# Delta stage of a two-layer kernel: the decay's distance as an absolute value on ScalarE, with work orders of their own for prologue and last head

## The chip, the cores and the metric

One core of one Trainium2 chip runs the whole program in one launch. The metric is the time of an execution in microseconds; three runs of the kernel before were timed, and one more was taken with the hardware profiler. Times inside the program are microseconds from the start of the profiled span.

## The reference

The program computes two transformer layers for B = 2 sequences of S = 512 rows with D = 256 columns, all in float32. Each layer adds a mixer and a mixture of experts, each behind a layer norm. The change touches only the first mixer, a gated delta rule with 16 key heads and 32 value heads of 128:

```python
mixed = silu(causal_conv1d(x @ w_qkv, conv_w))      # 4 taps
q, k, v = split(mixed)                              # q, k l2-normalised, each shared by 2 value heads
g = -exp(A_log) * softplus(x @ w_a + dt_bias);  beta = sigmoid(x @ w_b)
St = St * exp(g_t)                                  # one step per row t
delta = (v_t - k_t @ St) * beta_t
St = St + outer(k_t, delta);  o_t = q_t @ St
out = (rmsnorm(o) * norm_weight * silu(x @ w_z)) @ w_out
```

The kernel does it in chunks of 128 rows. Inside a chunk it needs, for rows j <= i, the decay exp(G_i - G_j), where G is the running sum of g (which is never positive, so that G falls with the row). As a full 128x128 matrix with both signs of the distance turned to the same one this is exp(-|G_i - G_j|): the mask of the later products throws away the half that isn't wanted.

## The kernel before

`build` (L2194) runs its phases one after the other: norm and gates (`phase_norm`, `phase_gates`, which also writes the running sums G of all heads to DRAM as rows), then `phase_delta` (L399), then the experts, attention and the second experts. Each phase is a block in which every engine has its own in-order program, and semaphores tie them together.

In `phase_delta` a head (one key head with its two value heads, both sequences; U = 4 units) passes through two halves. The preparation: eight convolutions (`conv` on TensorE, read out by `conv_r`, L785, as one plain and one scaled copy on ScalarE, three taps `tapa`, `tapb`, `tapc`, L926, on VectorE, `silu`, L794, on ScalarE), transposes `queries`, `keys`, `vals` with their read-outs, sums of squares `qsq` and `ksq` (four squares each), the gate products `gate`, the scalars `nscal` (L677) on GpSimd, and per chunk c = 0 to 3 the decay: `row` (L616) on SyncE fetches G of the chunk broadcast to all partitions (256 KB), `gap` (L710) turns it into the distance, `dexp` (L843) into the decay `dT`, `gram` multiplies keys with keys and queries, `mt` and `at` (VectorE) take the decay in, `cm` (GpSimd) and `nl` (VectorE) apply scale and mask, and `am` (GpSimd) masks `dT`. The 16x16 diagonal blocks of `nl` go through DRAM to a layout of lanes (`gath`, `gathr`), are inverted there in 13 steps `lane0` to `lane12` on VectorE, and come back (`putx`, `puty` behind a transposed copy `yl` on ScalarE, `scaty`, `scatx`). The second half, the recurrence: three levels of merges of the blocks (`v`, `m`, `y`, `a`, `xa`, `xb`), and per chunk `recall`, `rhs`, `solve`, `dl`, `ds`, `update`, `st`, `recallq`, `qs`, `output`, `o`, then norm and projection (`square`, `factor`, `oz`, `corev`, `core`, `core_r`, `project`, `project_r`). Stages without an engine named here are TensorE's if they are products, and else VectorE's or ScalarE's copies.

The order in which each engine runs its stages is written out by hand in one table `WINDOW` (L334) of 230 names. An engine's program is this table with only its own stages kept, so moving a name moves that stage on its one engine, and the distance between names of different engines means nothing. The table pairs the recurrence of head H with the preparation of head H + 1. It is used 15 times; the prologue (head 0's preparation, `PRO`) is the table with only preparation stages, the last head (`LAST`) with only recurrence stages (L375). In the last head every `v` and `y` starts with four idle products of 256 columns. Two PSUM banks `pp` go round among all users of `BANK_USERS` in the table's order, so a stage that takes a bank waits until the one two turns before is read out. At the start of each window SyncE's `head` (L595) waits until the window before has filled its last bank, then fetches the weights of head H + 2 (776 KB) and an output weight, and then come the four `row`.

The distance is two GpSimd operations per chunk, over 128x512: subtraction (L717) and a product with a table of signs (L719):

```python
pool.tensor_tensor(d, rows[p][:], over(hs[s][:, GRID, units(c)], 2, P), ALU.subtract).then_inc(s_gap, 1)
pool.wait_ge(s_gap, 2 * (CH * at.PH + c) + 1)
pool.tensor_tensor(d, d, over(k.c(C_SIGN), 1, U), ALU.mult).then_inc(s_gap, 1)
```

The weights of head 0 and 1 are fetched at the start of `phase_delta` (L590, L591), ahead of the first rows, which also wait until GpSimd has cleared 13 tiles (`s_zero`).

## Time and profile before

| | |
|---|---|
| three runs, median (lowest to highest) | 1699.26 us (1699.21 to 1701.25) |
| the profiled execution, own time | 1702.14 us |
| its span, mean granted TensorE clock | 1700.3 us, 0.953 of full speed |
| busy: TensorE, VectorE, GpSimd, ScalarE | 93%, 72%, 53%, 51% |
| delta stage | from about 39.5 to 1226 us |

The page gives each engine's busy share of the whole span; the prologue, the windows and the last head have different limits, so the timeline and the waits are read stretch by stretch. A timeline row gives start, duration, engine, line, operation, written and read tiles, shapes and how many instructions were merged into the row; in brackets the idle time before it and what ended it. "issue" means that no releaser was found. Matmul durations contain the pipeline's latency: stages follow each other faster than the durations add up, so the time of a stage is read from its start to the next one's.

### The profile page before, as it was taken

Reading aid. Unit: us, or ns where it says so; the run is one execution under the profiler, and the core shown is the slowest. Engines: PE = TensorE matmul, PEld = TensorE weight load, DVE = VectorE, ACT = ScalarE, POOL = GpSimd, SP = SyncE. Lnnn points to the kernel's source line nnn. Section 1 sums busy time; section 2 is a strip of 40 time slices with the busy share of each in tenths; the row PEclk is TensorE's granted clock in tenths of the full one; section 3 lists DMA queues with packets and bytes.
Section 4 is the critical chain, followed back from the end, with each engine's and each line's share of the span. In section 5 each row is a group of like instructions: output and inputs, shape, how many; then the busy total and the mean of one; then the engine's idle time right before and its main releaser. Section 6 shows DMA issues by size and latency. Waiting matters only on the chain. (4 is left out here: it accounts for less than half of the span.)

```text
span 1700.3 us, 28667 instructions
## 1 busy us (share of the span) xinstructions
PE 1587.0 (93%) x9280; PEld 1168.9 (69%) x9280; DVE 1216.5 (72%) x2565; ACT 860.2 (51%) x2367; POOL 908.4 (53%) x1101
## 2 busy tenths in 40 slices
PE   2689999999999999999999999999899899997997
PEld 2368778777787777877778777777655455555675
DVE  5679888898897978989788788894354354434445
ACT  1646757667576675766757667572311123341121
POOL 1647668686676866768668686672400112231332
PEclk8889999999999999999999999999999977778999
DMA  1120220201202012020120201200021360000413
GB/s 51 60 67 10 59 55 20 62 14 55 59 16 62 14 55 61 14 62 14 54 61 14 62 15 53 49 8 12 1 81 38 130 232 1 1 1 10 147 53 109
DMA packets 128642, 82.58 MB, mean 49 GB/s; under 512 B 92304, under 2 KB 110992, under 8 KB 128368
## 3 DMA queue, kind: packets, MB, share of 16 engines
q1 hardware_dynamic: 125152, 73.52, 15.4%
q0 software_dynamic: 2256, 6.18, 1.0%
q8 instruction: 78, 1.28, 0.3%
q10 hardware_dynamic: 1088, 1.05, 0.2%
q14 instruction: 68, 0.56, 0.1%
HBM read 62.97 MB, written 17.74 MB: 47 GB/s over the span
## 5 line engine op out<-in xcount | busy, mean ns | idle before, releaser
L926 DVE SCALAR_TENSOR_TENSOR dr_acc<-dr_raw,dr_wh,dr_acc 128x512 f32<-128x512 f32 x384 | 363.5, 960 | 46.1 <-ACT dr_acc L792 42.1
L1138 PE MATMUL dr_pp<-xnT,dr_wh 128*128 128x512 f32 x512 | 243.5, 609 | 6.0 <-DMA dr_wh<-in_w_head 5.4
L1138 PEld LDWEIGHTS dr_pp<-xnT,dr_wh 128*128 128x128 f32 x512 | 93.1, 194 | 88.6 <-issue 72.1
L1218 PEld LDWEIGHTS dr_pI<-dr_V,dr_X 128*64 128x64 f32 (+1 forms) x1536 | 125.3, 156 | 40.4 <-issue 30.5
L717 POOL TENSOR_TENSOR dr_dT<-dr_rows,dr_hs 128x512 f32<-128x512 f32 x64 | 76.5, 1195 | 134.2 <-issue 119.6
L1200 PEld LDWEIGHTS dr_pI<-dr_Y,dr_nl 128*64 128x64 f32 (+1 forms) x1536 | 125.5, 156 | 17.9 <-issue 13.5
L1170 PE MATMUL dr_pp<-dr_wh,xnT 128*128 128x256 f32 x512 | 124.5, 387 | 12.6 <-DVE x L1118 6.6
L1218 PE MATMUL dr_pI<-dr_V,dr_X 128*64 128x64 f32 (+1 forms) x1536 | 134.5, 242 | 0.2 <-DVE dr_V L1056 0.2
L1200 PE MATMUL dr_pI<-dr_Y,dr_nl 128*64 128x64 f32 (+1 forms) x1536 | 132.4, 240 | 1.7 <-DMA dr_Y<-dr_blocks_y 1.5
L791 ACT ACTIVATE dr_raw<-dr_pp 128x512 f32<-128x512 f32 x128 | 75.9, 593 | 107.2 <-PE dr_pp L1138 68.1
L1290 PE MATMUL dr_pp<-dr_wo,xn 128*128 128x256 f32 x512 | 124.3, 386 | 3.6 <-issue 1.8
L744 POOL TENSOR_TENSOR dr_ds<-dr_dl,dr_hs 128x512 f32<-128x512 f32 x48 | 62.4, 1299 | 120.4 <-ACT dr_dl L892 120.4
L756 POOL TENSOR_TENSOR xn<-xn,dr_zs 128x512 f32<-128x512 f32 x64 | 95.7, 1496 | 43.6 <-DVE xn L1113 34.0
L1170 PEld LDWEIGHTS dr_pp<-dr_wh,xnT 128*128 128x128 f32 x512 | 95.8, 193 | 29.7 <-DVE x L1118 10.1
L1960 POOL TENSOR_SCALAR_AFFINE_SELECT at_pT<-at_pT 128x128 f32<-128x128 f32 x128 | 36.1, 292 | 143.6 <-ACT at_pT L2107 142.3
L1290 PEld LDWEIGHTS dr_pp<-dr_wo,xn 128*128 128x128 f32 x512 | 94.3, 192 | 18.6 <-ACT xn L908 5.4
L719 POOL TENSOR_TENSOR dr_dT<-dr_dT,cst 128x512 f32<-128x512 f32 x64 | 94.7, 1480 | 5.0
L900 ACT ACTIVATE xn<-xn 128x128 f32<-128x128 f32 x256 | 75.7, 297 | 34.2 <-POOL dr_fac L770 19.1
L2107 ACT ACTIVATE at_pT<-at_u 128x512 f32<-128x512 f32 (+3 forms) x128 | 50.7, 444 | 73.7 <-PE at_u L2025 73.4
L732 POOL TENSOR_TENSOR dr_dT<-dr_dT,cst 128x512 f32<-128x512 f32 x64 | 80.8, 1283 | 13.0 <-DVE dr_dT L967 13.0
L792 ACT ACTIVATE dr_acc<-dr_pp,dr_wh 128x512 f32<-128x512 f32 x128 | 87.1, 680 | 0.0
L2015 PE MATMUL at_u<-at_kT,at_qT 32*128 32x512 f32 (+3 forms) x256 | 83.5, 583 | 0.2 <-DVE at_mx L2153 0.2
(292 smaller groups left out, 3736.3 us busy)
## 6 DMA issues: line engine op xcount, KB each, us to landing
dr_rows<-gt_rows SPq DMA_DIRECT2D x64, 256.0 KB, 3.5
dr_wh<-in_w_head SPq DMA_DIRECT2D x16, 776.0 KB, 4.6
ex_w<-in_moe SPq DMA_DIRECT2D x18, 608.0 KB, 11.1
dr_wo<-in_w_out SPq DMA_DIRECT2D x16, 256.0 KB, 4.7
dr_sorted_x<-ex_zero SPq DMA_DIRECT2D x1, 3999.0 KB, 29.5
so_xt<-dr_sorted_x SPq DMA_DIRECT2D x3, 1032.0 KB, 9.3
m_w<-in_moe SPq DMA_DIRECT2D x8, 384.0 KB, 3.1
dr_blocks_l<-dr_nl SPq DMA_DIRECT2D x128, 16.0 KB, 1.7
```

Source lines behind the costliest of these rows:

```text
L717: pool.tensor_tensor(d, rows[p][:], over(hs[s][:, GRID, units(c)], 2, P), ALU.subtract).then_inc(s_gap, 1)
L719: pool.tensor_tensor(d, d, over(k.c(C_SIGN), 1, U), ALU.mult).then_inc(s_gap, 1)
L732: pool.tensor_tensor(d, d, over(k.c(C_LE), 1, U), ALU.mult).then_inc(s_am, 1)
L756: pool.tensor_tensor(core[:].rearrange("p (b v) d -> p b v d", b=B), o[:].rearrange("p (b v) d -> p b v d", b=B), z, ALU.mult).then_inc(s_ ...
L792: act.activation(acc[q][:], flat(ps), ACT.Identity, scale=wh[at.ps][:, tap:tap + 1]).then_inc(free, 1)
L926: dve.scalar_tensor_tensor(acc[q][:], raw[q][:, w:w + S], wh[at.ps][:, col:col + 1], acc[q][:], ALU.mult, ALU.add).then_inc(done[q], 1)
L1138: mm = pe.matmul(flat(ps), wh[at.ps][:, w0:w0 + P], k.xnT[:, kt, b * S:(b + 1) * S], start=(kt == 0), stop=(kt == KT - 1))
L1170: mm = pe.matmul(ps[:, 2 * a:2 * a + 2].rearrange("p a b -> p (a b)"), k.xnT[:, kt, n * P:(n + 1) * P], wh[at.ps][:, w0:w0 + REP * DH], st ...
L1200: mm = pe.matmul(pairs(h, s)[rows, u], above(g, l), odd(Y[at.s][:, g:g + 1], s)[:, 0], start=True, stop=True)
L1218: mm = pe.matmul(pairs(h, s)[rows, u].rearrange("p m s -> p (m s)"), left[:, h * HU + u], V[h][:, u], start=True, stop=True)
L1290: mm = pe.matmul(ps[:, 2 * b:2 * b + 2].rearrange("p a b -> p (a b)"), cT[:, REP * b + w], wo[s][:, w], start=(w == 0), stop=(w == REP - 1))
L2015: pe.matmul(ps[:, 0:(qt + 1) * P], qT[Q % 2][rows, t0:t0 + P], kT[Q % 2][rows, b * S:b * S + (qt + 1) * P], start=True, stop=True).then_in ...
```

## The change

`gap` moves from GpSimd to ScalarE: four activations of 128x128 with the absolute value, scale -1 and the column of G as bias, |G_i - row|, instead of the two GpSimd operations; the exponential takes the minus sign as its scale. The table of signs leaves the constants. `WINDOW` is written anew; `PRO` and `LAST` become tables of their own. The weights of head 0 are fetched in the first norm phase, with a tile that lives longer. Cut to the core (the new tables stand whole, of the old `WINDOW` the start and the end):

```diff
                 sp.dma_start(k.alog[:], a_log_dram.partition_broadcast(P)).then_inc(k.s_gates, 16)
+                sp.dma_start(k.wh0[:], w_head_dram[0]).then_inc(k.s_wh0, 16)
                 sp.dma_start(k.router0[:], router_dram.rearrange("(k p) e -> p k e", p=P)).then_inc(k.s_router0, 16)
...
+PRO = """
+scal row0 yz conv1 conv0 conv_r1 tapa1 tapb1 tapc1 row1 conv3 conv_r0 conv2 gap0 silu1 tapa0 tapb0 tapc0 conv_r3
+tapa3 tapb3 queries1 tapc3 silu0 conv_r2 queries0 qsq1 tapa2 silu3 qsq0 tapb2 keys1 tapc2 keys_r1 silu2 keys0 ksq1
+keys_r0 ksq0 nscal gap1 gram0 gram1 row2 cm0 dexp0 dexp1 mt0 conv5 at0 conv4 gram2 gap2 dexp2 mt1 row3 at1 mt2
+gram3 nl0 cm1 gap3 dexp3 nl1 mt3 conv_r4 cm2 cm3 conv_r5 nl2 nl3 tapa5 tapb5 at2 gate0 tapa4 gath tapb4 conv7 tapc5
+gate_r0 silu5 at3 conv_r7 tapc4 gate2 tapa7 am0 tapb7 gate3 gathr lane0 lane1 gate_r2 gate1 gate_r1 silu4 gate_r3
+lane2 lane3 lane4 am1 conv6 lane5 vals1 lane6 lane7 lane8 lane9 lane10 lane11 conv_r6 lane12 tapc7 yl tapa6 tapb6
+vals_r1 am2 putx silu7 puty scaty tapc6 vals0 silu6 vals3 vals_r0 vals2 vals_r3 vals_r2 am3 scatx
+""".split()
 WINDOW = """
-conv1 row0 scal conv_r1 row1 conv0 gap0 conv_r0 tapa1 tapb1 tapc1 tapa0 conv3 tapb0 gap1 v0 silu1 conv_r3 m0 row2
-tapc0 silu0 conv2 conv_r2 tapa3 dexp0 y0 tapb3 queries0 a0 qsq0 tapc3 xa0 v1 tapa2 v2 dexp1 m2 conv5 y2 row3 m1 y1
...
-dl3 output3 oz2 lane6 lane7 gate_r0 lane8 corev2 lane9 core2 project_r1 o3 oz3 lane10 gate2 lane11 core_r2 square3
-lane12 at2 gate_r2 project2 factor3 corev3 gate1 yl tapc7 putx puty project_r2 vals2 gate_r1 silu7 at3 core3
-vals_r2 vals3 am1 vals_r3 core_r3 project3 scaty am2 project_r3 scatx am3
+scal conv1 conv_r1 tapa1 row0 conv0 tapb1 conv_r0 conv3 tapc1 tapa0 silu1 tapb0 v0 m0 conv_r3 tapa3 gap0 tapc0 v1
+y0 dexp0 m1 a0 row1 conv2 gap1 v2 yz silu0 tapb3 row2 tapc3 xa0 m2 silu3 y1 conv_r2 keys1 y2 keys_r1 a2 a1 xa1
+conv5 ksq1 queries0 tapa2 conv_r5 tapb2 v4 m4 v3 xb0 y4 tapc2 row3 qsq0 m3 silu2 tapa5 y3 keys0 a4 a3 keys_r0
+solve0 dl0 ds0 gram0 queries1 output0 ksq0 tapb5 qsq1 mt0 gram1 update0 tapc5 dexp1 gap2 o0 at0 conv4 conv_r4 st0
+xb1 gap3 recall1 mt1 nscal dexp2 v5 rhs1 tapa4 recallq1 cm0 solve1 at1 m5 dl1 gram2 qs1 cm1 dexp3 tapb4 ds1 tapc4
+gram3 nl0 mt2 square0 conv6 silu4 nl1 update1 y5 cm2 silu5 mt3 st1 oz0 nl2 conv_r6 a5 cm3 nl3 factor0 gath output1
+o1 vals0 square1 recall2 rhs2 conv7 solve2 tapa6 vals_r0 at2 conv_r7 tapb6 dl2 gathr tapc6 recallq2 corev0 tapa7
+factor1 qs2 ds2 vals1 core0 output2 oz1 vals_r1 o2 update2 corev1 core_r0 project0 st2 core1 core_r1 project_r0
+recall3 square2 am0 recallq3 project1 lane0 lane1 rhs3 oz2 solve3 qs3 dl3 gate0 lane2 silu6 lane3 factor2 lane4
+project_r1 lane5 lane6 corev2 am1 lane7 gate_r0 lane8 am2 output3 o3 core2 gate3 core_r2 oz3 lane9 lane10 gate2
+gate_r3 lane11 lane12 project2 square3 tapb7 gate_r2 factor3 project_r2 tapc7 yl corev3 gate1 vals2 vals_r2 gate_r1
+silu7 core3 core_r3 vals3 putx puty vals_r3 project3 at3 scaty am3 scatx project_r3
+""".split()
+LAST = """
+v0 v1 m0 m1 y0 a0 y1 xa0 v2 a1 m2 y2 a2 v4 v3 xb0 xa1 m3 m4 y4 a4 y3 a3 solve0 dl0 ds0 v5 output0 update0 o0
+square0 m5 st0 recall1 rhs1 xb1 solve1 y5 dl1 ds1 recallq1 a5 update1 oz0 factor0 corev0 qs1 output1 st1 recall2 o1
+rhs2 recallq2 square1 core0 core_r0 solve2 project0 dl2 oz1 project_r0 ds2 update2 factor1 qs2 st2 output2 recall3
+corev1 o2 core1 oz2 rhs3 square2 factor2 core_r1 recallq3 solve3 qs3 dl3 corev2 output3 o3 core2 square3 project1
+project_r1 core_r2 oz3 project2 factor3 corev3 core3 project_r2 core_r3 project3 project_r3
 """.split()
...
             sp.dma_start(nw[:], norm_w_dram.rearrange("(p a) -> p a", a=1)).then_inc(s_nw, 16)
-            load_w(w_head_dram[0:1], 0)
             load_w(w_head_dram[1:2], 1)
...
                 sp.wait_ge(k.s_rows, 16)
-                wait(sp, s_gap, 2 * (CH * at.PH + c - 2) + 1)
+                wait(sp, s_gap, CH * at.PH + c - 1)
                 sp.dma_start(flat(rows[p]), k.rows_dram[at.PH, c].partition_broadcast(P)).then_inc(s_rows[p], 16)
...
 
-            def gap(at, c):
-
-                s, p = at.ps, c % 2
-                pool.wait_ge(s_hs, at.PH + 1)
-                pool.wait_ge(s_rows[p], 16 * (2 * at.PH + c // 2 + 1))
-                wait(pool, s_O, CH * (at.H - 1) + c + 1)
-                d = dT[s][:, c]
-                pool.tensor_tensor(d, rows[p][:], over(hs[s][:, GRID, units(c)], 2, P), ALU.subtract).then_inc(s_gap, 1)
-                pool.wait_ge(s_gap, 2 * (CH * at.PH + c) + 1)
-                pool.tensor_tensor(d, d, over(k.c(C_SIGN), 1, U), ALU.mult).then_inc(s_gap, 1)
-
             def cm_(at, c):
...
 
+            def gap(at, c):
+
+                s, p = at.ps, c % 2
+                act.wait_ge(s_hs, at.PH + 1)
+                act.wait_ge(s_rows[p], 16 * (2 * at.PH + c // 2 + 1))
+                wait(act, s_O, CH * (at.H - 1) + c + 1)
+                for u in range(U):
+                    own = hs[s][:, GRID, c * U + u:c * U + u + 1]
+                    ins = act.activation(dT[s][:, c, u], rows[p][:, u], ACT.Abs, bias=own, scale=-1.0)
+                ins.then_inc(s_gap, 1)
+
             def dexp(at, c):
-                act.wait_ge(s_gap, 2 * (CH * at.PH + c) + 2)
-                act.activation(dT[at.ps][:, c], dT[at.ps][:, c], ACT.Exp).then_inc(s_dt, 1)
+                act.wait_ge(s_gap, CH * at.PH + c + 1)
+                act.activation(dT[at.ps][:, c], dT[at.ps][:, c], ACT.Exp, scale=-1.0).then_inc(s_dt, 1)
 
...
-                nc.sbuf_tensor("sc_rows", [P, 2, P], F32) as sc_rows:
+                nc.sbuf_tensor("sc_rows", [P, 2, P], F32) as sc_rows, nc.sbuf_tensor("wh0", [P, WROW], F32) as k.wh0:
-                                                         "in_router0", "in_router_bias")))
+                                                         "in_router0", "in_router_bias", "in_w_head")))
```

## Rows read from the trace of the kernel before

**Rows 1.** The page: busy us, share of the span, instructions

```profile
PE 1587.0 (93%) x9280; PEld 1168.9 (69%) x9280; DVE 1216.5 (72%) x2565; ACT 860.2 (51%) x2367; POOL 908.4 (53%) x1101
```

**Rows 2.** Waits of TensorE, 130 to 1120 us: us in total, times, longest

```profile
PE dr_pp L1170 <- DVE x L1118: 6.1, 14, 0.4
```

**Rows 3.** Timeline of TensorE at the starts of windows 1 and 14

```profile
174.47 1.88 PE L1138 MATMUL dr_pp<-xnT,dr_wh 128*128 128x512 f32 x4
...
1090.66 3.60 PE L1138 MATMUL dr_pp<-xnT,dr_wh 128*128 128x512 f32 x8
```

**Rows 4.** Groups by line, 130 to 1120 us: busy us, mean ns, idle before

```profile
L719 POOL TENSOR_TENSOR dr_dT<-dr_dT,cst 128x512 f32<-128x512 f32 x56 | 82.7, 1476 | 4.4
...
L717 POOL TENSOR_TENSOR dr_dT<-dr_rows,dr_hs 128x512 f32<-128x512 f32 x56 | 66.4, 1185 | 119.6 <-issue 119.6
...
L884 ACT ACTIVATE dr_qs<-dr_pB,dr_hs 128x128 f32<-128x128 f32 x168 | 47.7, 370 | 15.9 <-PE dr_pB L1235 15.9
...
L803 ACT ACT_TABLE_LOAD x28 | 35.9, 1283 | 0.5
...
L826 ACT ACTIVATE dr_tmp<-dr_ktok 128x128 f32<-128x128 f32 x116 | 34.4, 297 | 0.9
```

**Rows 5.** Timeline at the start of window 7, all engines, and window 14's first distance

```profile
597.29 5.31 PE L1138 MATMUL dr_pp<-xnT,dr_wh 128*128 128x512 f32 x12
...
600.53 10.74 SPq L620 DMA_DIRECT2D dr_rows<-gt_rows  x4
...
602.45 1.90 PE L1200 MATMUL dr_pI<-dr_Y,dr_nl 128*128 128x64 f32 x16
...
604.07 0.68 ACT L792 ACTIVATE dr_acc<-dr_pp,dr_wh 128x512 f32<-128x512 f32 x1
...
605.95 1.89 PE L1218 MATMUL dr_pI<-dr_V,dr_X 128*128 128x64 f32 x16
...
606.98 1.10 POOL L717 TENSOR_TENSOR dr_dT<-dr_rows,dr_hs 128x512 f32<-128x512 f32 x1 [9.53 <-issue]
...
608.12 2.97 PE L1200 MATMUL dr_pI<-dr_Y,dr_nl 128*128 128x64 f32 x32
...
1098.14 1.04 POOL L717 TENSOR_TENSOR dr_dT<-dr_rows,dr_hs 128x512 f32<-128x512 f32 x1 [7.33 <-issue]
```

**Rows 6.** Timeline of ScalarE in window 6

```profile
541.77 0.63 ACT L845 ACTIVATE dr_dT<-dr_dT 128x512 f32<-128x512 f32 x1 [1.60 <-POOL dr_dT L719]
...
543.71 0.63 ACT L803 ACTIVATE dr_kq<-dr_acc 128x512 f32<-128x512 f32 x1
```

**Rows 7.** Timeline of TensorE at the end of window 6

```profile
587.77 1.99 PE L1170 MATMUL dr_pp<-dr_wh,xnT 128*128 128x256 f32 x8 [0.43 <-DVE x L1118]
...
591.33 1.89 PE L1170 MATMUL dr_pp<-dr_wh,xnT 128*128 128x256 f32 x8
```

**Rows 8.** Timeline of the prologue, all engines

```profile
44.19 8.99 PE L1138 MATMUL dr_pp<-xnT,dr_wh 128*128 128x512 f32 x16 [5.39 <-DMA dr_wh<-in_w_head]
...
48.37 1.04 POOL L717 TENSOR_TENSOR dr_dT<-dr_rows,dr_hs 128x512 f32<-128x512 f32 x1 [3.65 <-DMA dr_rows<-gt_rows]
...
71.85 0.22 POOL L688 TENSOR_TENSOR dr_ssq_e<-dr_ssq,dr_c_eps 128x16 f32<-128x16 f32 x1 [9.07 <-ACT dr_tmp L826]
...
77.57 2.04 POOL L725 TENSOR_TENSOR dr_cm<-cst,dr_nck 128x512 f32<-128x512 f32 x2
...
85.61 3.76 SPq L628 DMA_DIRECT2D dr_blocks_l<-dr_nl  x8
...
98.99 0.34 SPq L637 DMA_DIRECT2D dr_blocks_x<-dr_T  x1
...
101.91 7.35 PE L1138 MATMUL dr_pp<-xnT,dr_wh 128*128 128x512 f32 x12
```

**Rows 9.** Timeline of the last head, TensorE

```profile
1164.17 2.00 PE L1200 MATMUL dr_pI<-dr_Y,dr_nl 128*128 128x64 f32 x16 [1.54 <-DMA dr_Y<-dr_blocks_y]
...
1213.84 1.05 PE L1261 MATMUL dr_pB<-dr_dl,dr_dT 128*128 128x128 f32 x8
```

More of the change, by code:

```diff
@@ L55 @@
 MAXE = 32
-C_SIGN = C_IOTA + MAXE
-C_GTP = C_SIGN + P
+C_GTP = C_IOTA + MAXE
 C_TOKEN = C_GTP + P
@@ L76, in constants @@
         c[:, C_LEVEL + l * HALF:C_LEVEL + (l + 1) * HALF] = (at[:, None] // s) == 2 * (col[None, :] // s)
-    c[:, C_SIGN:C_SIGN + P] = np.where(r[:, None] <= r[None, :], 1.0, -1.0)
     c[:, C_GTP:C_GTP + P] = c[:, C_GT:C_GT + P][:, order]
@@ L114, in __init__ @@
                                                      for n in ("gates", "router0", "rows"))
+        self.s_wh0 = ctx.enter_context(nc.semaphore("dr_w0"))
         self.rows_dram = nc.dram_tensor("gt_rows", [HK, CH, U * P], F32).ap()
@@ L141, in phase_norm @@
         if load:
-            x_dram, cst_dram, w_ab_dram, dt_bias_dram, a_log_dram, router_dram, bias_dram = load
+            x_dram, cst_dram, w_ab_dram, dt_bias_dram, a_log_dram, router_dram, bias_dram, w_head_dram = load
             @block.sync
@@ L339 @@
-o0 conv_r4 a3 tapa4 recall1 v5 recallq1 dexp2 rhs1 solve1 nscal tapb4 mt2 cm0 xb1 m5 cm1 square0 nl0 tapc4 dl1
-dexp3 conv6 gram3 ds1 qs1 mt3 cm2 nl1 y5 update1 silu4 output1 a5 oz0 conv7 st1 cm3 nl2 factor0 conv_r6 nl3 conv_r7
-recall2 gate3 o1 square1 rhs2 solve2 tapa7 gate_r3 vals0 dl2 corev0 ds2 vals1 recallq2 tapa6 vals_r0 tapb6 qs2
-tapb7 core0 oz1 gath factor1 vals_r1 update2 output2 tapc6 core_r0 silu6 st2 o2 project0 corev1 square2 gathr lane0
-recall3 project_r0 lane1 lane2 recallq3 core1 core_r1 gate0 rhs3 am0 solve3 lane3 lane4 factor2 qs3 lane5 project1
@@ L347 @@
+corev1 o2 core1 oz2 rhs3 square2 factor2 core_r1 recallq3 solve3 qs3 dl3 corev2 output3 o3 core2 square3 project1
+project_r1 core_r2 oz3 project2 factor3 corev3 core3 project_r2 core_r3 project3 project_r3
 """.split()
 CONVS = [(t, b) for t in range(NTILE) for b in range(B)]
-TURN_STAGES = ("v", "m", "y", "a", "xa", "xb", "recall", "recallq", "rhs", "qs", "solve", "dl", "ds", "output", "o",
-               "update", "st", "square", "factor", "oz", "corev", "core", "core_r", "project", "project_r")
@@ L367, in kept @@
     return 32 * KEPT.index(n // 2) + BLK * (n % 2)
-def turns(name):
-    return stem(name) in TURN_STAGES
-PRO = [x for x in WINDOW if not turns(x)]
-LAST = [x for x in WINDOW if turns(x)]
 def bank_uses(order):
@@ L409, in sem @@
             return ctx.enter_context(nc.semaphore(f"dr_{name}"))
-        wh = [sb(f"wh{i}", [P, WROW]) for i in range(2)]
+        wh = [k.wh0, sb("wh1", [P, WROW])]
         wo = [sb(f"wo{i}", [P, REP, D]) for i in range(2)]
@@ L486, in phase_delta @@
         s_free = [sem(f"free{i}") for i in range(NPP)]
-        s_w = [sem(f"w{i}") for i in range(2)]
+        s_w = [k.s_wh0, sem("w1")]
         s_wo = [sem(f"wo{i}") for i in range(2)]
@@ L776, in corev @@
                 pool.tensor_tensor(core[:], core[:], over(fac[:], 2, DH), ALU.mult).then_inc(s_core, 1)
-            run(pool, {"am": am, "nscal": nscal, "gap": gap, "cm": cm_, "yz": yz, "ds": ds_,
+            run(pool, {"am": am, "nscal": nscal, "cm": cm_, "yz": yz, "ds": ds_,
                        "factor": factor, "oz": oz, "corev": corev})
@@ L811, in summing @@
             def summing(at, name):
-                order = [n for n in WINDOW if stem(n) in ("ksq", "qsq")]
+                order = [n for n in (PRO if at.kind == "pro" else WINDOW) if stem(n) in ("ksq", "qsq")]
                 before = order[:order.index(name)]
@@ L908, in core_r @@
                 act.activation(cT[:], ps[:], ACT.Identity, scale=nw[:]).then_inc(free, 1)
-            run(act, {"conv_r": conv_r, "silu": silu, "keys_r": keys_r, "ksq": ksq, "qsq": qsq, "gate_r": gate_r, "dexp": dexp,
+            run(act, {"conv_r": conv_r, "silu": silu, "keys_r": keys_r, "ksq": ksq, "qsq": qsq, "gate_r": gate_r, "gap": gap, "dexp": dexp,
                       "yl": turned, "m": m, "a": a, "qs": qs_, "dl": dl_, "square": square, "core_r": core_r})
```

2 lines of the change are left out of this document (removed).

## The prediction

> **What bounds the kernel now.** I read the page first: TensorE is busy 93% of the span [rows 1]. All that the change touches lies in the delta stage, which ends near 1226 us; the rest of the program keeps its 474 us. The delta stage has three parts: a prologue that prepares head 0 with nothing beside it, 15 full windows (head H's recurrence beside head H+1's preparation) and the last head alone. Of these, the waits of TensorE were the next view: in 990 us of full windows it waits for other engines 6.3 us, nearly all for one addition of VectorE, once a window [rows 2]. TensorE bounds them. The starts of windows 1 and 14 give the period, (1090.66 - 174.47)/13 = 70.48 us [rows 3]. Its stages back to back would take about 68; the rest hides as short waits for PSUM banks near the window's end. So in the windows only a changed order or a new wait counts, while the prologue and the last head are chains of latencies, where each step counts.
>
> **The GpSimd work removed.** Two operations per chunk, 1185 + 1476 ns [rows 4], 10.6 us a window. They run beside a full TensorE and GpSimd is 53% busy: worth nothing by themselves; if TensorE were not full, they would be worth at most what the next engine, VectorE (72%), allows.
>
> **The ScalarE work added.** 16 absolute values of 128x128 a head. The trace has no such operation. The nearest row is the per-column scaling of 128x128, four of which take 1.14 us by a mean of 370 ns with overlap [rows 4]; bounds: 0.9 (four at 297 ns less overlap, the squares' row) and 1.5 (four at 370 without). 4.6 us a window on an engine that is 51% busy; only its place matters. The minus signs of the exponential and of the scale are free fields. Table loads: a full window changes between exponential and SiLU four times before and four times after; the prologue five times before, three after. I take it that absolute value, like the squares and copies, needs no load of its own.
> What the four loads cost is read behind an exponential: it ends at 541.77 + 0.63 = 542.40 and the SiLU behind the load starts at 543.71 [rows 6], so 1.31 us with the load's own 1.28 [rows 4] for the change, nothing more. The Trainium skill (ScalarE: Activation LUTs, What ACT_TABLE_LOAD costs) wants about 1.38 us of drain beside the 1.28; the trace disagrees, and by the page the two loads at a window's front would make its SiLU 2.8 us later.
>
> **The window's front.** This is where the change adds a wait: ScalarE, in order, now stands at the first distance until the first row broadcast lands, and behind it are the exponential, the second distance and the SiLUs of tiles 0 and 3, for which TensorE's transposes of keys 1 wait. Before, only GpSimd stood there. In window 7 the rows are asked for at 600.53 and used at 606.98, 9.7 us after the start at 597.29; in window 14 7.5 us after (1098.14 against 1090.66, [rows 3, 5]); the other windows from 1 on lie between, 8.7 on average. ScalarE gets there at 604.07 + 0.68, +7.5 [rows 5]. In the new order the inversion lanes end about 0.8 us earlier against the window's end, and through the transposed copy and SyncE's scatters the row request comes 0.5 earlier: rows at +8.15. Then distance 1.14, load 1.3, exponential 0.63, distance 1.14, load 1.3, two SiLUs 1.2: +14.9. TensorE comes to keys 1 after three convolutions 5.16, one convolution and a first merge stage 3.50, three more such stages 5.2 and a short one 1.17 (both from the 32-matmul row, [rows 5]): +15.0. Just in time; each window whose rows come later than +8.25 waits for the excess, 0.2 us on average. If the wait stays as late as in window 7, it is 1.4.
>
> **The rest of the window.** I laid TensorE's stages of the new order end to end and hung the others' on them. One more place is short: output 2 needs ScalarE's scaling of chunk 2, which stands behind the convolution read-out and the copy of the deltas: 0.4 us. At the end the old order waits 0.43 us for the projection's addition before a gate stage [rows 7], and from the last gate stage at 591.33 it needs 5.96 us to the next start at 597.29, though its stages are 1.73 + 3 x 0.46 + 1.72 = 4.8 long [rows 5, 7]: waits of 1.1 us. With the shorter transposes and bank turns around them the end loses about 2.0 us. The new order has four stages between the projection 1 and the bank's next use, so the first wait goes; at the end about 0.9 remains, and 0.3 of small ones. Per window: -0.8 + 0.2 + 0.4 = -0.2 us, bounds -1.0 and +0.8; 15 windows: **-3**.
>
> SyncE's requests for rows 2 and 3 now wait for distances 0 and 1 on ScalarE and land microseconds ahead of theirs; nothing but the block gather stands behind them.
>
> **The prologue.** Head 0's weights (776 KB) are now asked for at the program's start, behind x, the constants (64 KB fewer) and the gates' inputs; only the router's weights, needed after the delta stage, are pushed back: 0. Before, TensorE waited 5.39 us for them [rows 8]. Nothing shows that the block opens before about 39.5, so the first convolution moves from 44.19 to 39.5. But the first distance waits on ScalarE for rows that land at 48.37 as before [rows 8], since SyncE asks for them behind GpSimd's memsets. So ScalarE goes on at 48.4 + 1.14 = 49.5. From there to the last sum of squares it has one load 1.28, four SiLUs 2.5, two read-outs 2.4, four groups of four squares 4.8 (297 ns each with a short accumulator read, [rows 4]) and two key copies 1.2: 61.7. These sums release GpSimd's scalars, at 71.85 before [rows 8]: -10. Behind them come 5.7 us of scalars (71.85 to 77.57, the first mask product, [rows 8]), the products and the exponentials, now in one batch with one load; the block gather starts near 73.5 instead of 85.61, and the lanes end near 87.5 instead of 98.99 [rows 8]. The new order then leaves seven VectorE operations, 5.0 us, where 2.9 passed before: the first full window starts at 92.4 instead of 101.91, **-9.5**. Bounds: -4.5, if only the weights' wait is gained, and -12.
>
> **The last head.** Today it starts with a wait of 1.54 us for the scattered blocks, until 1164.17 [rows 9]; with earlier lanes about 0.7 less. The new table reaches the same second recall, but then puts update 2 ahead of the projection, and output 3 ahead of projection 1: output 3, at 1213.84 today [rows 9], comes about 2.4 us earlier, and everything behind it hangs on it. **-2.4**, bounds 0 and -3.5.
>
> **Sum.** -9.5 - 3 - 2.4 = -15 us. The profiled execution took 1702.1 (span 1700.3), giving 1687; the median of the runs is 2.9 lower, so 1684.
>
> **The rivals.** (a) *ScalarE's wait decides the windows, slower than before.* Rows stay as late as in window 7, or the distance costs its upper bound, and what stands behind it (SiLU 2, the exponentials ahead of the masks) misses its stages too. At 1.7 us a window, +25 against -12: 1712. It turns slower above 0.8 us a window, so from rows later than about +9.0. For it: six of the fourteen lie there today. Against: a late window start moves the rows' request no further, so the wait limits itself. 0.11. (b) *The prologue gains only its first wait*, because memory round trips and VectorE's taps bound it: 1691 with windows unchanged or slightly worse; with windows 0.5 us longer nothing is left, 1698. 0.20, a quarter of it within 0.2%. (c) *The windows gain more*: the end of the window loses its waits and the front has none, -1.0 each: 1672. 0.15. (d) *The absolute value asks for another table*, so the change isn't what it says: two more loads at the front, 2.6 us a window, 39 - 12: 1726. Nothing in the trace shows it; squares, copies and scalings stand between both tables without a load. 0.02. The Trainium skill (ScalarE: Activation LUTs, Table sets: the hidden batching unit) lists absolute value among the cheap functions of every set, which speaks against it.
>
> **How the numbers follow.** Forecast 0.52, (b) 0.20, (c) 0.15, (a) 0.11, (d) 0.02. Changes within 0.2% (3.4 us) are what a measurement of this kernel can hardly tell from none. Faster: 0.52 + 0.15 + 0.15 = 0.82; same: 0.05 from (b) and 0.02 from (a) near its turning point; slower 0.11. The forecast's own range is 1678 to 1690; with (c) and (b) it becomes 1670 to 1697.
>
> **What would show it.** Right: first full window at 91 to 94; its period 70.0 to 70.6; no TensorE wait for the weights; scalars at about 62 in the prologue; gate stages without the 0.43 us wait; last block of the delta stage 2 us shorter. Wrong: a TensorE wait of a microsecond for a SiLU at keys 1 in each window (a), table loads of more than 56 in 14 windows (d), scalars later than 66 (b).

## The result, and the profile after: slower by 2.9%

Median 1751.0 us (1743.1 to 1754.1, 4 runs) against 1700.3 us (1699.2 to 1702.4, 4 runs) for the kernel before in the same runs: ratio 1.029, 95% interval 1.026 to 1.032. I had forecast 1684 us, with 1670 to 1697 as the range. The profiled execution of the changed kernel took 1743.1 us, the fastest of its four runs and 41.0 more than the one of before (1702.1); the medians lie 50.7 apart, so the traces show the smaller loss.

The page of the changed kernel, busy us, share and instructions (before: [rows 1]):

```profile
PE 1578.3 (91%) x9280; PEld 1166.2 (67%) x9280; DVE 1211.3 (70%) x2565; ACT 922.8 (53%) x2621; POOL 738.0 (42%) x973
```

GpSimd lost 170 us of work and ScalarE gained 63, as meant. No other engine became full; TensorE's own work is the same within 1%, but it stands still more often. The waits of TensorE in 990 us of full windows (total, times, longest; before: [rows 2]) show it:

```profile
PE dr_pp L1294 <- DVE dr_vtok L951: 19.3, 14, 1.4
PE dr_pA L1274 <- POOL dr_ds L737: 12.5, 14, 1.2
PE dr_pB L1265 <- ACT dr_qs L888: 9.3, 14, 0.8
PE dr_pp L1157 <- ACT dr_kq L796: 5.0, 9, 1.1
PE dr_pA L1254 <- DVE dr_rhs L1091: 4.8, 14, 0.3
PE dr_pp L1282 <- ACT dr_zs L833: 4.4, 13, 0.3
PE dr_pp L1164 <- ACT dr_vT L796: 3.9, 13, 0.3
```

Up to seven places in a window where there was one: 59 us instead of 6. TensorE's first convolutions of windows 1 and 14 (before: [rows 3]) stand at

```profile
173.92 5.31 PE L1142 MATMUL dr_pp<-xnT,wh 128*128 128x512 f32 x12
...
1131.69 3.60 PE L1142 MATMUL dr_pp<-xnT,dr_wh 128*128 128x512 f32 x8
```

a period of (1131.69 - 173.92)/13 = 73.67 us instead of 70.48: 3.2 x 15 = 48 us, about the whole loss. To see where in the window, I cut it at three events on TensorE: the first turn's first stage (v0), solve 1, and the first projection. Window 6 before, then the same window after with the waits between solve 1 and the projection:

```profile
531.95 1.89 PE L1200 MATMUL dr_pI<-dr_Y,dr_nl 128*128 128x64 f32 x16
...
561.32 1.05 PE L1250 MATMUL dr_pA<-dr_rhs,dr_Y 128*128 128x128 f32 x8
...
577.28 1.89 PE L1290 MATMUL dr_pp<-dr_wo,xn 128*128 128x256 f32 x8
...
602.45 0.78 PE L1200 MATMUL dr_pI<-dr_Y,dr_nl 128*128 128x64 f32 x6
```

```profile
546.78 3.68 PE L1204 MATMUL dr_pI<-dr_Y,dr_nl 128*128 128x64 f32 x32
...
575.32 1.05 PE L1254 MATMUL dr_pA<-dr_rhs,dr_Y 128*128 128x128 f32 x8
...
580.69 1.13 PE L1274 MATMUL dr_pA<-dr_ds,dr_ktok 128*128 128x256 f32 x4 [0.87 <-POOL dr_ds L737]
...
587.34 1.13 PE L1254 MATMUL dr_pA<-dr_rhs,dr_Y 128*128 128x128 f32 x8 [0.34 <-DVE dr_rhs L1091]
...
591.05 1.13 PE L1265 MATMUL dr_pB<-dr_dl,dr_dT 128*128 128x128 f32 x8 [0.66 <-ACT dr_qs L888]
...
594.43 1.99 PE L1294 MATMUL dr_pp<-dr_wo,xn 128*128 128x256 f32 x8 [1.39 <-DVE dr_vtok L951]
...
620.40 0.78 PE L1204 MATMUL dr_pI<-dr_Y,dr_nl 128*128 128x64 f32 x6
```

Before: 29.37 + 15.96 + 25.17 us. After: 28.54 + 19.11 + 25.97. The middle stretch holds as much TensorE work as before (19.11 - 3.26 of waits = 15.85 against 15.96); it is longer by the four waits shown. Who is late there, on VectorE and GpSimd of the changed kernel:

```profile
578.30 1.44 DVE L977 TENSOR_TENSOR dr_nl<-dr_nl,dr_cm 128x512 f32<-128x512 f32 x1 [1.00 <-POOL dr_cm L718]
...
584.86 0.69 DVE L977 TENSOR_TENSOR dr_nl<-dr_nl,dr_cm 128x512 f32<-128x512 f32 x1 [1.00 <-POOL dr_cm L718]
...
589.76 4.01 DVE L930 SCALAR_TENSOR_TENSOR dr_acc<-dr_raw,dr_wh,dr_acc 128x512 f32<-128x512 f32 x3
...
593.70 0.68 DVE L951 TENSOR_TENSOR dr_vtok<-dr_pp,dr_vsc 128x512 f32<-128x512 f32 x1
```

```profile
576.67 2.52 POOL L718 TENSOR_TENSOR dr_cm<-cst,dr_nck 128x512 f32<-128x512 f32 x2
...
579.15 1.48 POOL L737 TENSOR_TENSOR dr_ds<-dr_dl,dr_hs 128x512 f32<-128x512 f32 x1
...
582.04 1.27 POOL L749 TENSOR_TENSOR xn<-xn,dr_zs 128x512 f32<-128x512 f32 x1
...
583.28 1.49 POOL L718 TENSOR_TENSOR dr_cm<-cst,dr_nck 128x512 f32<-128x512 f32 x1
```

The scaled solution (L737), for which update 1 waits, stands behind two coefficient tables; the fourth table stands behind the gate's product (L749), and VectorE waits for it ahead of output 1's sum; the eviction that frees the projection's bank (L951) stands behind three taps of 1.34 us each. Nowhere among these is the distance. So the trace gave a first theory of my own, against the obvious one: T1, the new order of the full window makes the loss; T2, the distance on ScalarE makes it. A third, T3, is that VectorE and GpSimd slow each other where they work side by side.

### The profile page after: what moved, and what is told of

Same layout as the page of the kernel before. It is cut to its first block and busy times, and to the rows that moved or that the text cites. A ratio compares the mean times of both kernels' runs of the same rounds, so it can differ in the third digit from the quotient of the medians.

```text
span 1741.4 us, 28825 instructions
## 1 busy us (share of the span) xinstructions
PE 1578.3 (91%) x9280; PEld 1166.2 (67%) x9280; DVE 1211.3 (70%) x2565; ACT 922.8 (53%) x2621; POOL 738.0 (42%) x973
## 3 DMA queue, kind: packets, MB, share of 16 engines
q8 instruction: 78, 1.28, 0.3%
## 5 line engine op out<-in xcount | busy, mean ns | idle before, releaser
L737 POOL TENSOR_TENSOR dr_ds<-dr_dl,dr_hs 128x512 f32<-128x512 f32 x48 | 56.5, 1176 | 398.7 <-ACT dr_dl L896 398.7
L930 DVE SCALAR_TENSOR_TENSOR dr_acc<-dr_raw,wh,dr_acc 128x512 f32<-128x512 f32 x192 | 166.4, 877 | 26.3 <-ACT dr_acc L785 23.7
L930 DVE SCALAR_TENSOR_TENSOR dr_acc<-dr_raw,dr_wh,dr_acc 128x512 f32<-128x512 f32 x192 | 167.6, 883 | 21.2 <-ACT dr_acc L785 18.6
L1142 PE MATMUL dr_pp<-xnT,wh 128*128 128x512 f32 x256 | 119.1, 599 | 2.4 <-ACT dr_zs L833 1.7
L1142 PE MATMUL dr_pp<-xnT,dr_wh 128*128 128x512 f32 x256 | 120.8, 605 | 0.0
L749 POOL TENSOR_TENSOR xn<-xn,dr_zs 128x512 f32<-128x512 f32 x64 | 99.0, 1547 | 41.8 <-PE dr_pp L1282 21.5
L784 ACT ACTIVATE dr_raw<-dr_pp 128x512 f32<-128x512 f32 x128 | 75.2, 587 | 73.8 <-PE dr_pp L1142 60.5
L725 POOL TENSOR_TENSOR dr_dT<-dr_dT,cst 128x512 f32<-128x512 f32 x64 | 83.4, 1314 | 54.8 <-DVE dr_dT L971 54.8
L912 ACT ACTIVATE xn<-dr_pp,dr_nw 128x512 f32<-128x512 f32 x64 | 44.4, 694 | 98.3 <-PE dr_pp L1282 97.3
L844 ACT ACTIVATE dr_dT<-dr_rows,dr_hs 128x128 f32<-128x128 f32 x256 | 81.2, 389 | 21.7 <-issue 17.3
L718 POOL TENSOR_TENSOR dr_cm<-cst,dr_nck 128x512 f32<-128x512 f32 x64 | 86.2, 1357 | 1.9 <-DVE dr_nl L977 0.7
L977 DVE TENSOR_TENSOR dr_nl<-dr_nl,dr_cm 128x512 f32<-128x512 f32 x64 | 63.6, 996 | 30.6 <-POOL dr_cm L718 30.6
```

The costliest lines, as they stand in the source:

```text
L718: pool.tensor_tensor(cm[p][:], over(k.c(C_GTP), 1, U), over(nck[s][:, units(c)], 2, P), ALU.mult).then_inc(s_cm[p], 1)
L725: pool.tensor_tensor(d, d, over(k.c(C_LE), 1, U), ALU.mult).then_inc(s_am, 1)
L749: pool.tensor_tensor(core[:].rearrange("p (b v) d -> p b v d", b=B), o[:].rearrange("p (b v) d -> p b v d", b=B), z, ALU.mult).then_inc(s_ ...
L784: act.activation(raw[q][:, TAPS - 1:], flat(ps), ACT.Copy)
L844: ins = act.activation(dT[s][:, c, u], rows[p][:, u], ACT.Abs, bias=own, scale=-1.0)
L930: dve.scalar_tensor_tensor(acc[q][:], raw[q][:, w:w + S], wh[at.ps][:, col:col + 1], acc[q][:], ALU.mult, ALU.add).then_inc(done[q], 1)
```

## The experiments

Ratios are to the kernel before, run on the same chip beside each; its own median moved between 1700 and 1707 us from chip to chip, so times are compared through the ratio. The period comes from one profiled execution, as above, from the starts of windows 1 and 14. Windows with the same order and the distance on GpSimd (before, e1, e2, e12) have periods of 70.5 to 70.8 us, so a difference of 0.3 us between two periods says nothing by itself. "Old order" is the order of before.

**Taking the change apart.** Four kernels:

```
e1  before + first head's weights asked for in the opening stage
e2  changed; WINDOW = old; GpSimd distance in full windows only
e3  changed; WINDOW = old, "gap" right ahead of its "dexp" (on ScalarE)
e4  changed; WINDOW = new; GpSimd distance in full windows only
```

> The kernel before, with one part of the change alone: the first head's weights are asked for in the opening stage, ahead of the router's weights; tables and distance are those of before. In the changed kernel the opening stage shrank by about 2.9 us (first window's scalars at 99.05 instead of 101.91). If the early weights alone bring that gain: 1700.3 - 3 = about 1697 us; if what I predicted for them holds and the new order of the prologue lost part of it again: the 5.39 us wait for the weights goes and about 1.5 us of other waits come, so about 1696 us. If they bring nothing, because the rest of the prologue hangs on GpSimd: 1700 us. No theory of the windows says anything of this run: its window period must stay at 70.5 us.

> The changed kernel with the window's order of before and the distance on GpSimd in the full windows (two operations each, as before); the prologue's and the last head's own tables, the early weights and the distance on ScalarE in the prologue stay as changed. Both theories of the windows (T1: the new order of the in-order queues makes the loss; T2: the distance on ScalarE makes it) expect the period to fall from 73.7 back to 70.5 us: 1751 - 15 x 3.2 = 1703, and by the traces' prologue (-2.9) and last head (+1.2) beside the kernel before 1698.6 us. If the loss were outside the full windows, 1740 or more.

> The changed kernel with the window's order of before, each distance put on ScalarE right ahead of its exponential. It tells the theories apart. T1 (the new order of the queues of GpSimd and VectorE makes the loss): period 70.5 to 71.2 us, 1698 to 1710 us. T2 (the distance on ScalarE, its 5 us of extra work per window and its wait for the row of sums, makes the loss): period 73 us or more, 1740 us or more. T3 (VectorE and GpSimd slow each other down because they work side by side more): as T1 if the order is what puts them side by side.

> The changed kernel with its new tables, but in the full windows the distance is made by two GpSimd operations again (at the places where the new order has it). T1 (order makes the loss): the period stays at 73.7 us or gets longer, since GpSimd has four pairs of 1.48 + 1.19 us more: 1751 to 1790 us. T2 (the distance on ScalarE makes it): period back to about 70.5, 1700 to 1710 us.

| kernel | window's order | distance in windows | ratio (95%) | mean period, us |
|---|---|---|---|---|
| e1 | old | GpSimd | 0.996 (0.993 to 0.999) | 70.8 |
| e2 | old | GpSimd | 0.997 (0.995 to 0.999) | 70.7 |
| e3 | old | ScalarE | 0.998 (0.995 to 1.001) | 70.8 |
| changed | new | ScalarE | 1.029 (1.026 to 1.032) | 73.7 |
| e4 | new | GpSimd | 1.043 (1.037 to 1.049) | 76.2 |

In e1 the first convolution starts at 40.6 us and the first window's scalars (`scal`, a copy of VectorE) are at 96.8, 6.0 earlier than before; the ratio says 7 us, with 2 to 12 inside its interval, against the 3 to 4 that I expected. Of the 6.0 us, 3.6 are the earlier start. Another 1.9 are the first sixteen products themselves: behind the wait for the weights they took 8.99 us before, at a mean granted clock of 0.79 (between the levels of 1.2 and 2.4 GHz), and 7.11 us in e1, at 1.00 (2.4 GHz). Its period came out at 70.8, not at the 70.5 that I had said must stay, with nothing changed in the windows: that is the spread named above.

T1 holds and T2 falls, on both sides (e3 and the changed kernel differ in the window's table alone): with the old order the distance on ScalarE costs next to nothing, and with the new order the distance on GpSimd makes it worse. The waits of e3, then of e4, in the same 990 us:

```profile
PE dr_pp L1175 <- DVE x L1123: 6.1, 14, 0.4
PE dr_pI L1205 <- ACT dr_Y L876: 3.6, 14, 0.3
```

```profile
PE dr_pA L1297 <- POOL dr_ds L757: 42.9, 13, 3.3
PE dr_pp L1317 <- DVE dr_vtok L974: 10.8, 13, 1.4
```

In the new order GpSimd's queue is short of time: with its distances in it, TensorE's wait for the scaled solution grows from 0.9 to 3.3 us a window.

**The distance alone**, prologue included, nothing else changed, and **what should pay, alone** (e12 = e1 with the new `LAST`):

> The kernel before with the distance alone changed: one absolute value per gate unit on ScalarE, right ahead of its exponential, in the prologue too; no early weights, all three orders those of before. The runs so far say that GpSimd's relief is worth nothing, since no wait of TensorE hung on it, and that ScalarE's extra 5 us per window bring a wait of 0.26 us: period 70.6 to 71.0 instead of 70.5 us, ratio 1.000 to 1.005. If the relief of GpSimd were worth something (the ranking of my prediction, 0.2 us less per window), ratio 0.998 or less.

> What of the change should pay, alone: early weights, and the last head's own order; the distance stays on GpSimd, prologue and window keep their orders. Early weights gave ratio 0.996 (first convolution at 40.6 instead of 44.2 us, first window at 96.8 instead of 102.8); the last head's order gave 0.2 to 0.8 us at equal clock, and would at best give 1.8 us. So ratio 0.994 to 0.996. If the last head's order is worth nothing: level with early weights alone.

e11: ratio 1.004 (1.002 to 1.006), period 70.8. The edit that gives the change its name loses a little: TensorE waits for ScalarE's copy of Y in each window, 4.0 us in 14 windows, or 0.29 each. The stretch from the first stage to solve 1 shows it too: in window 6 it takes 29.70 to 29.71 us in e3, e8 and e11, and 29.37 to 29.42 with the distance on GpSimd (before, e1, e2, e12). 0.3 us times 15 is 4 to 5 of the 7 us. e12: 0.9935 (0.991 to 0.996), the lowest ratio of all; its interval overlaps e1's, so that the last head's order adds anything is not shown. **e8** keeps the distance on ScalarE beside early weights and the new `LAST`, with old orders else:

> The change without its new orders of prologue and window: distance on ScalarE everywhere, right ahead of its exponential in the orders of before, early weights, and the last head's own order. The runs so far put the new prologue's order at 3 us lost (from the first convolution to the first window 59.5 us against 56.1 with early weights and the old order), the early weights at 5 to 6 us gained, and the last head's order at 0.2 to 0.8 us gained at equal clock. So it should stand 5 to 7 us below the kernel before: ratio 0.996 to 0.997, level with early weights alone. If the distance on ScalarE costs the windows anything (e3 showed a wait of 0.26 us per window for dr_Y), up to 4 us of that is lost: ratio 0.999.

Ratio 1.000 (0.997 to 1.003), against 0.9935 for e12, which differs from e8 in the distances alone: on ScalarE they take back what the early weights bring.

**Repairing one queue of the new order.** e5 moves two items of GpSimd's queue, e6 one of VectorE's, e7 both:

```
e5  GpSimd:   nscal cm0 ds1 cm1 cm2 cm3 oz0    (was: nscal cm0 cm1 ds1 cm2 oz0 cm3)
e6  VectorE:  vals_r0 at2 vals_r1 tapb6 tapc6 tapa7    (was: ... tapb6 tapc6 tapa7 vals_r1)
```

> The changed kernel; in the new window's order only GpSimd's queue is altered: the scaled solution of chunk 1 goes ahead of the second coefficient table, and the fourth coefficient table ahead of chunk 0's product with the gate. TensorE's, ScalarE's and VectorE's queues stay. The trace shows update 1 waiting 0.87 us for that scaled solution and VectorE 1.00 us for the fourth table, ahead of output 1's sum. T1a (the queue of GpSimd makes a part of the loss by itself): both waits go, the period falls by 0.9 to 1.9 us, 1722 to 1738 us. R (the window lacks work between the turns, and a wait that is taken away comes back one step later): period less than 0.4 us shorter, 1745 us or more.

> The changed kernel; in the new window's order only VectorE's queue is altered: the eviction of values 1, which gives back the accumulator bank that the first projection needs, goes ahead of three taps (4.0 us) instead of behind them. T1b (VectorE's queue makes a part of the loss by itself): the first projection's wait of 1.39 us (19.3 us over 14 windows) goes, the period falls by 1.1 to 1.4 us, 1730 to 1735 us. R (waits move on): less than 0.4 us, 1745 us or more.

> The edits of the two kernels before it together. If the two parts are independent, the savings add up: period shorter by 2.3 to 3.2 us, 1703 to 1717 us, so that hardly anything of the loss of 48 us is left. R: less than 1 us, 1735 us or more.

Measured, in this order, 1.026 (1.021 to 1.030), 1.017 (1.014 to 1.021) and 1.022 (1.018 to 1.026), with periods of 74.7, 73.3 and 73.7 us. e6, and more narrowly e7, are below the changed kernel's 1.029 (1.026 to 1.032). A gain of e5 isn't shown: the intervals overlap, and its period, from the slowest of its four executions, is even longer. The rival I had called R comes nearer than T1a and T1b: the wait that I aimed at went, and another took its place. Among the waits of TensorE, of e5 (update 1's wait is gone, the next recall waits instead), then of e6 (the projection's wait is gone, recall 3 waits):

```profile
PE dr_pA L1231 <- DVE dr_st L1105: 12.7, 14, 1.0
```

```profile
PE dr_pA L1231 <- DVE dr_st L1105: 20.6, 14, 1.5
PE dr_pA L1275 <- POOL dr_ds L738: 12.5, 14, 1.2
```

In e7 both stand at the recalls, 34.2 us in all, so the savings don't add up. In e6 the state (L1105) now stands behind the three taps that the eviction went ahead of. Cut as above, window 6 of e6 has 28.00 + 17.57 + 27.61 us: the middle gave 1.5 back, the end took 1.6.

**Splices.** The window's order up to some stage from one table, what is left from the other; everything on ScalarE, prologue and last head as changed.

> The changed kernel, the full window's order spliced: up to solve 1 the order of before (distance ahead of its exponential), from there on what is left in the new order. The change's trace reaches solve 1 at 32.9 us of the window and 1.5 us ahead of the old order (34.4), and has 3.3 of its 4.2 us of waits between solve 1 and the first projection. S (the new order behind solve 1 makes the loss): period 73 us or more, ratio to before 1.020 or more. F (the new order of the first half makes it, since it leaves ScalarE, GpSimd and VectorE behind at solve 1): period 70.5 to 71.3, ratio below 1.006.

> The same splice the other way round: the new order up to solve 1, the old one behind it. S: period 70.5 to 71.3 us, ratio below 1.006. F: period 73 us or more, ratio 1.020 or more. If each half costs a part by itself, both splices lie between, and their losses add up to about the 3.2 us of the whole.

> The full window's order spliced later: the order of before up to the first projection, what is left in the new order; all else as changed. The splice at solve 1 (old, then new) kept the whole loss: period 73.75 us. If the loss is made between solve 1 and the first projection, where the change's trace has 3.3 of its 4.2 us of waits: period 70.6 to 71.3 us, ratio below 1.006. If it is made behind the first projection (TensorE needs 21.7 us from there to the next window's first turn against 20.5 us before): period 72 us or more.

> The order of before up to solve 3, the new order behind it (projection 1, output 3, the gates, the last two blocks of values). e13_split_project, spliced at the first projection, kept a period of 73.3 to 73.6 us. If the new order loses between the first projection and solve 3: period at most 71.5 us, ratio below 1.008. If it loses in the gates and values behind solve 3 (e13 waited 0.56 us at values 2 and 1.18 at chunk 3's transposes there): 72 us or more, ratio 1.012 or more.

> The order of before up to solve 1 and behind solve 3; between them the new order. With e3 (all old), e9 (new from solve 1 on) and e17 (new from solve 3 on) it closes a square: middle old or new, end old or new; periods so far 70.8 (old, old), 73.8 (new, new), 73.6 to 75.0 (old, new). If the middle carries a loss of its own, as the waits of the change's own trace say (3.3 us between solve 1 and the first projection): period 73 us or more, ratio 1.018 or more, and middle and end are two bottlenecks of which the longer counts, not the sum. If the middle's waits only take up what the end would take anyway: 71.5 us or less, ratio below 1.008.

| kernel | to solve 1 | solve 1 to first projection | to solve 3 | end | ratio (95%) | period |
|---|---|---|---|---|---|---|
| e3 | old | old | old | old | 0.998 (0.995 to 1.001) | 70.8 |
| e10 | new | old | old | old | 1.006 (1.002 to 1.009) | 71.6 |
| e9 | old | new | new | new | 1.024 (1.019 to 1.030) | 73.8 |
| e13 | old | old | new | new | 1.022 (1.018 to 1.025) | 73.6 |
| e17 | old | old | old | new | 1.029 (1.026 to 1.032) | 74.1 |
| e18 | old | new | new | old | 1.056 (1.051 to 1.062) | 77.4 |

e9 and e10 place the loss behind solve 1 (S, not F). e10's period is 0.8 us above e3's, a little more than S allowed, but that isn't lost in the first part: its window 6 reaches solve 1 1.4 us earlier than e3's (28.27 us against 29.70) and then waits for scaled queries of ScalarE:

```profile
PE dr_pB L1266 <- ACT dr_qs L889: 11.3, 14, 0.8
```

Beyond that the splices do not divide the loss: the new end alone keeps it all, the new middle alone makes it twice as large, and together they cost no more than the end alone. So it isn't two bottlenecks of which the longer counts either, as I had put it before e18: e18 is longer than both. The window of e17 runs like the old one up to the gates and then waits:

```profile
609.43 1.99 PE L1175 MATMUL dr_pp<-dr_wh,xnT 128*128 128x256 f32 x8 [1.62 <-ACT dr_zs L834]
611.97 0.66 PE L1165 MATMUL dr_pp<-cst,dr_vT 128*128 128x128 f32 x4 [0.54 <-DVE x L1123]
613.81 0.65 PE L1283 MATMUL dr_pp<-cst,xn 128*128 128x128 f32 x4 [1.18 <-POOL xn L770]
```

while e18 keeps the middle's waits (17.9 us at the first projection in 13 windows), and the one wait of the old order, for the projection's addition ahead of the gate's matmuls, grows from 0.4 to 2.2 us:

```profile
PE dr_pp L1175 <- DVE x L1123: 28.6, 13, 2.2
```

A splice behind solve 1 also splits what a table pairs: gate 3 is ahead of solve 2 in the old order and late in the new. In e18 it falls behind solve 3, beside gate 0, and there most of the extra time is: window 6 takes 18.08 us from solve 1 to the first projection, as in e9 (18.07), but 28.43 from there to its end, against 25.97 in e9 and 25.17 in e3. That is a limit of these runs: a splice shows where an order can't be exchanged, not what its part costs in place.

**Putting one block back.** Two guesses at that pair, and one at e13's:

```
e14  changed; gate3 ahead of solve2 (TensorE), gate_r3 ahead of dl2 (ScalarE)
e15  e14 + e6
e16  e13; core1 behind recallq3, project1 behind solve3
```

> The changed kernel with one block of TensorE's work moved back to where the old order has it: the gate's matmuls of tile 3 (1.9 us) ahead of solve 2, with their eviction ahead of solution 2's on ScalarE. L (the new order moved this filler out from between the turns, where the turns' chain now stands bare): the waits for the right-hand side, the scaled queries and the values' bank take it in, the period falls by 1.2 to 1.9 us, ratio 1.012 to 1.018. C (the chain through VectorE, with its taps, is what lasts, so 1.9 us more of TensorE work ahead of solve 2 pushes the chain back by as much): period within 0.4 us of 73.7, ratio 1.025 or more.

> The gate's matmuls moved back as in e14_gate_back and VectorE's eviction of values 1 moved ahead of its three taps as in e6_vector_queue, which alone gave 0.37 us per window. L: the two together give 1.6 to 2.3 us, ratio 1.008 to 1.014. C: no more than e6_vector_queue gave, ratio 1.016 to 1.020, with the wait now at recall 3 for the state.

> The kernel of e13_split_project (old order up to the first projection, new behind it) with chunk 1's transposes moved behind recall 3 and its queries, and its projection behind solve 3, on TensorE, as the old order has them. In e13 the transposes wait 1.61 us for GpSimd's product and the projections stand ahead of the last turn. If this placement makes the loss behind the first projection: period down from 73.3 to 71.0 to 72.2 us, ratio 1.004 to 1.013. If waits only move on along the chain: above 73 us, ratio 1.018 or more.

Measured, in this order, 1.043 (1.036 to 1.049), 1.066 (1.063 to 1.069) and 1.029 (1.025 to 1.034), with periods of 76.3, 78.5 and 74.1 us. L is refuted; C foretold no gain in e14, but not a loss of 2.6 us a window, and for e15 it expected what e6 gave, where the two edits together cost 4.8. The waits of e14:

```profile
PE dr_pp L1175 <- DVE dr_vtok L952: 29.9, 13, 2.3
PE dr_pp L1165 <- DVE x L1123: 15.9, 13, 1.2
```

Its first wait is 2.3 us of the moved gate stage itself: convolutions, values, gates, transposes and projections share two accumulator banks in turn, so one more stage ahead of solve 2 wants its bank before VectorE has evicted values 0. In e16 the wait went from the transposes to a right-hand side (22.3 us in 13 windows), as the second of its two expectations had it.

## Why the prediction was wrong, step by step

None of the times that I priced, the highest being rival (d)'s 1726 us, reached 1751.

**The work moved** was priced nearly right: nothing for GpSimd's relief, the four activations of a distance in 1.26 to 1.28 us where I took 1.14, and no table of its own for the absolute value, 27 + 26 table loads in 13.5 windows. Rival (d) is out. The Trainium skill (ScalarE: Activation LUTs, Table sets: the hidden batching unit) lists absolute value in every set, and the trace agrees:

```profile
L844 ACT ACTIVATE dr_dT<-dr_rows,dr_hs 128x128 f32<-128x128 f32 x216 | 68.5, 389 | 17.3 <-issue 17.3
...
L796 ACT ACT_TABLE_LOAD x27 | 34.6, 1283 | 0.5
L849 ACT ACT_TABLE_LOAD x26 | 33.4, 1283 | 0.5
```

**The window's front.** I gave ScalarE's wait 0.2 us a window; keys 1 waits 5.0 us in all, in nine of 14 windows, 0.36 on average. I had let the rows come 0.5 us earlier. They didn't: the first distance starts 8.7 us into the window on average of windows 1 to 14, as before, and not at 8.15. Rival (a), the likelier of the two slower ones, named this place and was wrong about it: the wait is a ninth of the loss.

**The rest of the window** is the step that failed: "-0.8 + 0.2 + 0.4 = -0.2 us", measured +3.2: by the stretches of window 6 -0.8 up to solve 1, +3.2 to the first projection and +0.8 behind it. What I named was near: output 2's wait 0.4, measured 0.66; the addition's 0.43 gone; at the end 0.3 + 0.3 left. What I didn't name was update 1 (0.87), solve 2 (0.34) and above all the first projection (1.39): 2.6 us a window. I had laid TensorE's stages end to end and looked up for each the instruction that releases it. I had not run GpSimd's and VectorE's queues forward in their new order: both waits of VectorE for a coefficient table and the eviction behind three taps are positions in a queue, to be read from the table. The bound of +0.8 for this term held nothing for them, so it excluded what happened. The taps also took 1.34 us each there, where their mean is 0.88. That these waits are what the loss consists of is read from the trace; that putting them right one by one would have saved it is not so, as e5 to e7 show.

**The prologue**, -9.5 forecast, -2.9 measured (first window's convolution 99.05 against 101.91 in [rows 8]):

```profile
40.35 7.10 PE L1142 MATMUL dr_pp<-xnT,wh 128*128 128x512 f32 x16 [0.73 <-PEq L209]
...
83.38 6.62 PE L1174 MATMUL dr_pp<-wh,xnT 128*128 128x256 f32 x16 [4.56 <-ACT dr_acc L785]
...
99.05 5.38 PE L1142 MATMUL dr_pp<-xnT,dr_wh 128*128 128x512 f32 x8
```

```profile
62.30 0.22 POOL L692 TENSOR_TENSOR dr_ssq_e<-dr_ssq,dr_c_eps 128x16 f32<-128x16 f32 x1 [14.55 <-ACT dr_tmp L819]
```

```profile
75.40 3.76 SPq L632 DMA_DIRECT2D dr_blocks_l<-dr_nl  x8
...
92.39 0.34 SPq L641 DMA_DIRECT2D dr_blocks_x<-dr_T  x1
```

The chain to the scalars was right (62.3, forecast 61.7) and to the gather nearly (75.4, 73.5). Behind it I let the lanes follow without the taps and read-outs between them, and they end at 92.4 instead of 87.5. The SiLU of tile 5 waits on ScalarE for VectorE's taps, the read-out of convolution 7 stands behind it, and the last two taps ahead of the lanes wait for this read-out:

```profile
81.41 0.63 ACT L796 ACTIVATE dr_vT<-dr_acc 128x512 f32<-128x512 f32 x1 [5.79 <-DVE dr_acc L930]
```

The lanes start at 85.0, 4.6 us behind the request for their blocks at 80.4; before, 2.0 us were enough (90.61 to 92.59). Then I counted VectorE's 5.0 us without TensorE's waits in between for banks and SiLUs, and 6.7 us passed. A part of the chain that gained 10 us was no longer the longest. The runs put a price on each part, from the first convolution to the first window's scalars: 56.1 us with early weights, old order and GpSimd's distance (e1, e12), 58.4 with ScalarE's distance instead (e8), 59.0 to 59.7 with the new order as well (changed, e2, e3). So the distance and the new order of the prologue give back 3 of the 6 us that the early weights bring. Rival (b) was nearest here, with a gain of the first wait alone and VectorE's taps among what bounds the rest.

**The last head**, -2.4 forecast. Output 3 comes 1258.56 - 1207.77 = 50.8 us behind the first stage instead of 49.7, since it waits 0.69 us for ScalarE and others ahead of it wait too; to the router's first matmul it is 72.13 us instead of 72.30, so nothing was gained:

```profile
1207.77 2.70 PE L1204 MATMUL dr_pI<-dr_Y,dr_nl 128*128 128x64 f32 x16 [1.90 <-DMA dr_Y<-dr_blocks_y]
...
1258.56 1.16 PE L1265 MATMUL dr_pB<-dr_dl,dr_dT 128*128 128x128 f32 x8 [0.69 <-ACT dr_dl L896]
...
1279.90 3.71 PE L1377 MATMUL m_ps_router<-router,xnT 128*128 128x12 f32 x32 [0.94 <-PEq L133]
```

```profile
1236.47 1.70 PE L1373 MATMUL m_ps_router<-router,xnT 128*128 128x12 f32 x14 [0.94 <-PEq L134]
```

**The sum** of the two traces: prologue -2.9, fifteen windows with the wait in front of the last head +46.5 (1207.77 - 99.05 against 1164.17 - 101.91), last head -0.2, the unchanged rest behind the router's first matmul -2.3: +41.1, the difference of the spans.

**What is shown and what stays open.** Shown: the window's order makes the loss, not the distance, and it is the order behind solve 1. Not settled: which single placement. Six kernels moved one to three placements each. Against the changed kernel e6 gained 1.1%, e7 0.7% and e5 nothing clear; e14 and e15 lost, and so did e16 against its own base e13. e7 put right at once the three late placements of GpSimd and VectorE named above, and three quarters of the loss stayed. I take from this that no single one makes it, which is argued, not shown; the scaled queries that output 2 waits for (0.66 us) were never moved. T3 is open as well, since the order is also what sets the two engines side by side; over the whole program VectorE's busy time did not rise (1216.5 us before, 1211.3 after).

## What to carry to other kernels

When a change rewrites a hand-made order, price it engine by engine: walk every in-order queue in its new sequence with the durations of the trace, not only the bound engine's stages with their releasers. That would have shown the waits; no run shows that it would have found a good order. Test the arithmetic edit and the reordering apart before anything else; here two small kernels (e3, e4) told them apart, and what was left of the change when the distance and the old prologue and window stayed (e12: early weights, the last head's order) made a kernel 0.65% faster than before. In this kernel a wait was a symptom: e5 to e7 took the longest ones away and most of the time came back at the next ones, and in e14 a stage moved ahead waited 2.3 us for an accumulator bank that it shares with stages it has no data in common with.
